# Expert blocks of 128 slots against pairs of 64-slot blocks whose second weights are fetched by number, in a decoder block on one core

## The chip, the core and the metric

The kernel runs on one core of a Trainium2 chip, which has an engine for matrix products (TensorE, PE in the profile), VectorE (DVE), ScalarE (ACT), GpSimd (POOL), and SyncE (SP), which issues most DMAs. Each engine runs its own instructions in order; semaphores connect them. The metric is the time of one execution on the device in microseconds.

## What is computed

One decoder block over 4 sequences of 1024 tokens of 256 numbers: linear attention, cross attention to 77 context tokens, and a feed-forward part (FFN). All 4096 tokens pass a gated FFN with a shared set of weights. 512 of them, given by index lists, also go to one of 8 experts (mixture of experts, MoE): the expert with the best score. Cut to the part that the change touches:

```
x_moe  = x[index_b, index_t]                         # 512 x 256
scores = sigmoid(x_moe @ eg_w.T + eg_b)              # 512 x 8
e      = argmax(scores + exp_bias)                   # an expert for each token
h1, h2 = x_moe @ ew1[e].T + eb1[e], x_moe @ ew2[e].T + eb2[e]
z      = layernorm(silu(h1) * h2) * g + b            # 512 x 128
y      = z @ ew3[e].T + eb3[e]                       # 512 x 256
out[index_b, index_t] = shared_ffn * shared_w + y * expert_w + residual
```

All numbers are float32.

## The kernel before

The first 297 us or so are the two attentions, tile by tile (32 tiles of 128 tokens). Behind them the FFN runs over *units* of four tiles, in the order of `UNITS` (line 43): F0 to F5 (dense units of 512 tokens), G (the 512 gathered tokens through the shared FFN), F6, F7, and the MoE units M0, M1, M2.

The gathered tokens are sorted by expert with rank products and a table. An expert's tokens take whole blocks of 128 slots; the worst case is `NBLK` = MT + NE - 1 = 4 + 7 = 11 blocks, and all 11 are computed always, padded or not. `choose_slots` (DVE) works out each token's slot, POOL scatters the token rows to these slots in memory (line 1761, semaphore `placed`), and SP reads the blocks back into the on-chip memory as `hs_in` (line 475, semaphore `hs_loaded`). `map_blocks` (DVE, a unit behind `choose_slots`) works out `block_i`, the expert's number of each block, and `block_hot`, with which a product adds the expert's bias. All 8 experts' weights (`we_12`, `we_3`) lie on the chip from early on, and PE picks a block's weights by a number that it reads from `block_i` into a register (`load_expert`, line 882: in the program a TENSOR_LOAD and two register instructions).

PE's order in a step q: `gate_products(q)` (for a MoE unit line 753, two products a block with the expert's weights as the moving operand, 256 columns each, and one for the bias, line 755), `z_features(q-1)` and `y_products(q-1)` (line 803, bias line 806), and `to_features(q+1)` (transposes of the next unit's tokens, line 489). At the step of F7 `to_features` of M0 stands at the end; it waits for `hs_loaded[0]`. A float32 product stands in the trace as two passes, so two products are x4 there.

Behind the MoE gate products, ACT makes the tanh (1036), DVE the product with it and the statistics (1322, 1327, 1332, 1336), POOL the reciprocal roots (`invert_blocks`, 1669 and 1672), and DVE normalises (1344). `y_evict` (DVE, 1301) adds the result to a row that other scatters prepared, and `scatter_blocks` (POOL, 1746) writes each block's rows to the output with one indirect DMA a block. The program ends when all of these have landed.

SP's order around it: the stores of the results of F0 to F5 (line 462); then the wait for `placed` and the three loads of `hs_in` (475); then the store of F6, the load of M0's prepared rows (`load_base`, 467), the two stores of F7, and the other loads of prepared rows.

Of the kernel before, what the change touches and what calls it, by code (L numbers as in the profile page):

```python
# [7 lines left out]
BF16 = mybir.dt.bfloat16  # L8
# [5 lines left out]
P = 128  # L14
# [9 lines left out]
HF = 128  # L24
# [15 lines left out]
NBLK = MT + NE - 1  # L40
# [21 lines left out]
def decoder_block(nc, A):  # L62
    ctx = ExitStack()
    with ctx:  # L64
# [143 lines left out]
        hs_in = wide_[:, 0:2816].rearrange("p (b d) -> p b d", b=NBLK)  # L208
# [3 lines left out]
        m_th, m_u, m_z = (wide_[:, n:n + 512].rearrange("p (j n) -> p j n", j=GT) for n in (9792, 10304, 10816))  # L212

# [5 lines left out]
        iota12 = sb("iota12", [P, 12])  # L219
        iota128 = sb("iota128", [P, MT])  # L220
        over = sb("over", [P, NE, MT])
# [7 lines left out]
        past = sb("past", [P, NBLK, NE])  # L229
        block_e = sb("block_e", [P, 12])  # L230
        block_i = sb("block_i", [P, 12], I32)
        block_oh = sb("block_oh", [BIAS_ROWS, NBLK, NE])
        block_sum = sb("block_sum", [BIAS_ROWS, 12])
        block_hot = sb("block_hot", [BIAS_ROWS, 12], BF16)
# [80 lines left out]
        scattered = sem("scattered")  # L315

# [22 lines left out]
        def is_tile(t):  # L339
            return 0 <= t < NT  # L340

# [50 lines left out]
        def _(sp):  # L392
# [94 lines left out]
        def _(pe):  # L487
# [242 lines left out]
            def gate_products(pe, n, half, expert=None, load_expert=None):  # L730
# [15 lines left out]
                else:  # L746
                    k = UNITS[n][1]
                    for j in range(2 * half, min(2 * half + 2, size(n))):
                        b = GT * k + j
                        dst = sbank[2 + half][:, (j % 2) * D:(j % 2 + 1) * D]  # L750
                        for ch in range(CH):
                            w = we_12[:, bass.ds(expert[b], 1), ch, :].rearrange("p o n -> p (o n)")
                            pe.matmul(dst, h3t[:, n % 2, ch, j * P:(j + 1) * P], w, start=(ch == 0), stop=False)  # L753

                        mm = pe.matmul(dst, block_hot[:, b:b + 1].to_broadcast([BIAS_ROWS, P]), be_16[:, 0:2 * HF],  # L755
                                       start=False, stop=True)
# [25 lines left out]
            def y_products(pe, n, expert=None, load_expert=None):  # L782
# [10 lines left out]
                for j in range(size(n)):  # L793

                    if is_moe(n) and j % 2 == 0:
                        wait(pe, ys_ready, GT * UNITS[n][1] - 2 + j)
                    if is_dense(n):
                        w = w_3c[:, :]
                    else:
                        wait(pe, mzt_ready, UNITS[n][1] + 1 + (j >= parts(n)[0][1]))  # L800
# [1039 lines left out]
```

## Time and profile before

| | us |
|---|---|
| median of 3 runs | 381.24 (380.94 to 381.77) |
| the profiled execution's own time | 381.03 |
| its span, first to last instruction | 379.1 |
| outside the span | 1.93 |
| last store of F0 to F5 issued by SP | 334.4 |
| `hs_in` loads issued | 339.46 |
| transposes of M0 on PE | from 343.4 |
| first and last scatter of results on POOL | 361.57 and 375.67 |

The profile is of one execution. A row of the timeline gives start and duration of a run of like instructions on an engine; durations of PE passes overlap their neighbours', so the distance between starts tells the pace. DMA issues count as work of the queue that issues them (SPq); a number given as "to landing" goes from the issue to the arrival.

### The profile page before, as it was taken

What the parts mean: (1) busy time and instruction counts of PE and PEld (TensorE: products, weight loads), DVE (VectorE), ACT (ScalarE), POOL (GpSimd) and SP (SyncE); (2) the same over time, 40 slices, a digit from 0 to 9 for tenths busy, and PEclk for the clock granted to TensorE, in tenths of its full rate; (3) what the DMA queues carried; (4) which work ended last, traced back from release to release, by engine and by line L of the source; (5) the groups of instructions that cost most, each with busy time, mean ns of one, the idle gap of its engine ahead of it and who ended that gap; (6) DMA issues with size and microseconds to landing.
All of it is one profiled execution on the core that took longest, in us unless ns stands there. A gap on an engine that the chain in (4) does not pass through costs nothing. (4 is left out here: it accounts for less than half of the span.)

```text
span 379.1 us, 10587 instructions
## 1 busy us (share of the span) xinstructions
PE 360.7 (95%) x3483; PEld 261.5 (69%) x3483; DVE 298.8 (79%) x934; ACT 164.3 (43%) x395; POOL 282.3 (74%) x417
## 2 busy tenths in 40 slices
PE   8999999999999999999999999999899989998971
PEld 4566677777777777767777777778676566656751
DVE  2588788898989898888898878886756598799771
ACT  1553553453455356436436524432456445341320
POOL 5338987766777866877867789898888888687385
PEclk9999999999999999999999999999999999999997
DMA  8994891300300120032221012003000223136630
GB/s 256 315 310 94 238 298 22 68 16 16 72 30 16 35 54 16 19 83 90 94 52 37 29 24 65 16 22 80 15 30 28 83 86 111 57 115 216 189 109 13
DMA packets 38076, 33.32 MB, mean 88 GB/s; under 512 B 4425, under 2 KB 37224, under 8 KB 38024
## 3 DMA queue, kind: packets, MB, share of 16 engines
q1 hardware_dynamic: 35016, 28.37, 26.4%
q0 software_dynamic: 1456, 3.37, 3.0%
q10 hardware_dynamic: 1552, 0.92, 0.9%
q8 instruction: 29, 0.48, 0.5%
q14 instruction: 23, 0.19, 0.2%
HBM read 15.58 MB, written 13.78 MB: 77 GB/s over the span
## 5 line engine op out<-in xcount | busy, mean ns | idle before, releaser
L1595 POOL TENSOR_TENSOR s_t<-s_t,causal 128x512 f32<-128x512 f32 x63 | 78.9, 1272 | 15.6 <-ACT s_t L909 15.4
L501 PE MATMUL bank<-h1t,w_qkv 128*128 128x512 f32 x112 | 52.9, 595 | 0.4 <-DVE x L1168 0.3
L1155 DVE TENSOR_TENSOR s_t<-sbank,causal 128x512 f32<-128x512 f32 x65 | 43.5, 671 | 1.1 <-PE sbank L522 1.0
L1587 POOL TENSOR_TENSOR state_wide<-state,own_pair 128x256 f32<-128x256 f32 x28 | 18.9, 675 | 25.5 <-DVE state L1146 24.4
L909 ACT ACTIVATE s_t<-sbank 128x512 f32<-128x512 f32 x63 | 33.7, 587 | 7.8 <-PE sbank L522 7.8
L522 PE MATMUL sbank<-arena 32*128 32x256 f32 x512 | 36.7, 400 | 0.0
L561 PE MATMUL bank<-s_t,vp 128*32 128x128 f32 x1024 | 34.6, 275 | 1.1 <-DVE s_t L1155 0.4
L508 PE MATMUL bank<-w_qkv,h1t 128*128 128x256 f32 x128 | 34.2, 389 | 0.0
L1603 POOL TENSOR_TENSOR rr<-ve,neg_half 128x3 f32<-128x3 f32 x36 | 31.9, 887 | 3.0
L646 PE MATMUL bank<-w_out,attn_t 128*128 128x256 f32 x128 | 33.6, 385 | 0.5 <-DVE attn_t L1236 0.5
L740 PE MATMUL sbank<-h1t,w 128*128 128x512 f32 x72 | 33.0, 596 | 0.5 <-ACT h1t L909 0.5
L1190 DVE BATCH_NORM_STATS2 stats<-x 128x6 f32<-128x256 f32 x87 | 31.6, 412 | 0.0
L1112 DVE TENSOR_SCALAR arena<-bank,b_qk 128x512 f32<-128x512 f32 x28 | 21.0, 751 | 13.1 <-PE bank L501 13.1
L909 ACT ACTIVATE prob_t<-bank 77x128 f32<-77x128 f32 x32 | 8.7, 273 | 50.2 <-PE bank L489 50.2
L561 PEld LDWEIGHTS bank<-s_t,vp 128*32 128x32 f32 x1024 | 26.2, 109 | 6.2 <-issue 2.1
L489 PEld LDWEIGHTS bank<-ident,h 128*128 128x128 f32 x128 | 17.6, 140 | 17.3 <-issue 12.4
L501 PEld LDWEIGHTS bank<-h1t,w_qkv 128*128 128x128 f32 x112 | 19.1, 190 | 14.2 <-issue 13.4
L968 ACT ACTIVATE prob<-sc,nmx 128x77 f32<-128x77 f32 x32 | 11.5, 360 | 37.9 <-DVE nmx L1220 37.9
L1614 POOL TENSOR_TENSOR x<-x,b_out 128x256 f32<-128x256 f32 x32 | 26.0, 813 | 0.0
L522 PEld LDWEIGHTS sbank<-arena 32*128 32x128 f32 x512 | 23.1, 184 | 3.9 <-issue 2.4
L646 PEld LDWEIGHTS bank<-w_out,attn_t 128*128 128x128 f32 x128 | 21.8, 190 | 3.5 <-DVE attn_t L1236 1.5
L489 PE MATMUL bank<-ident,h 128*128 128x128 f32 x128 | 24.2, 272 | 0.0
(215 smaller groups left out, 831.7 us busy)
## 6 DMA issues: line engine op xcount, KB each, us to landing
rden_t<-rden SPq DMA_DIRECT2D x64, 64.0 KB
rows<-x SPq DMA_DIRECT2D x32, 128.0 KB, 1.9
x<-in_x SPq DMA_DIRECT2D x7, 512.0 KB, 7.9
out<-x SPq DMA_DIRECT2D x7, 512.0 KB, 2.9
we<-in_we SPq DMA_DIRECT2D x1, 2048.0 KB
rows<-empty SPq DMA_DIRECT2D x1, 1419.0 KB, 6.4
rows<-empty SPq DMA_DIRECT2D x1, 1408.0 KB, 7.6
xmask<-in_mask POOLq DMA_DIRECT2D x2, 616.0 KB, 10.8
```

Of the source, the lines that this page charges most:

```text
L489: return pe.transpose(dst, src, ident[:, :])
L501: mm = pe.matmul(dst[:, :], w_qkv[:, ch, cb * P:(cb + 1) * P], h1t[:, g % 3, ch, :], start=(ch == 0), stop=(ch == CH - 1))
L508: mm = pe.matmul(v_place(t), h1t[:, (t // GT) % 3, ch, tok(t)], w_qkv[:, ch, 2 * D:3 * D], start=(ch == 0), stop=(ch == CH - 1))
L522: mm = pe.matmul(both, kt(slot, ch)[rows, tok(t)], qpair(slot, ch)[rows, :, tok(t)], start=True, stop=True)
L561: mm = pe.matmul(bank[3][32 * r:32 * r + 32, ch * P:(ch + 1) * P], v_of, s_t[:, r, 2 * ch + par, :], start=(first and ch + par == 0), stop ...
L646: mm = pe.matmul(bank[0][:, 0:D], attn_t[:, M % 2, ch, :], w_out[:, ch, :], start=(ch == 0), stop=(ch == CH - 1))
L740: mm = pe.matmul(sbank[2 + half][:, :], w_12[:, ch, half * HF:(half + 1) * HF], h3t[:, n % 2, ch, :], start=(ch == 0), stop=(ch == CH - 1))
L909: return act.activation(dst, src, ACT.Copy)
L1155: dve.tensor_tensor(s_t[:, r, :, :], sbank[r][:, :].rearrange("p (s q) -> p s q", s=4), causal[:, :].unsqueeze(1).to_broadcast([P, 4, P]), ...
L1190: last = dve.bn_stats(stats[:, k, :], x[:, t, :])
L1595: pool.tensor_tensor(s_t[:, r, :, :], s_t[:, r, :, :], causal[:, :].unsqueeze(1).to_broadcast([P, 4, P]), ALU.mult)\
L1603: pool.tensor_tensor(rr[:, i, :], ve[:, i, :], neg_half[:, 0:3], ALU.pow).then_inc(rr_ready, 1)
```

## The change

The unit of an expert's tokens becomes a block of 64 slots: worst case `NHALF` = 2·4 + 7 = 15. Two of them share the 128 partitions of one old block, so `NBLK` is 8 and there are two MoE units, M0 and M1, in place of three. The two halves may have different experts. Each product of a block becomes two products of 64 output partitions (`dst[0:64]` and `dst[64:128]`), which use 64 of the array's columns each: the first with weights picked by number from the resident `we_12` and `we_3`, the second with weights in a buffer of the pair's own, `we_odd[b]`. SP fills the 7 buffers from memory: for each it reads the expert's number from `block_i` into a register and issues two DMAs, 256 KB and 128 KB, whose source addresses come from the register. The buffers lie over tensors that are no longer in use. The tables (`over`, `past`, `block_e`, `block_oh`, ...) get 16 columns in place of 11 or 12. `map_blocks` is split in two functions that are called in a row at the step where it was called before.

```diff
-NBLK = MT + NE - 1
+HB = P // 2
+NHALF = 2 * MT + NE - 1
+NBLK = -(-NHALF // 2)
...
+        def odd_of(k):
+            return [b for b in blocks_of(k) if 2 * b + 1 < NHALF]
...
                 if n == GATHERED:
+                    sp.wait_ge(expert_ready, 1)
+                    for m in range(NMG):
+                        for b in odd_of(m):
+                            e = sp.value_load(block_i[0:1, 2 * b + 1:2 * b + 2], min_val=0, max_val=NE - 1)
+                            sp.dma_start(we_odd[b][:, 0:2 * CH * HF].rearrange("p (c n) -> p c n", c=CH),
+                                         A["we_12"][bass.ds(e, 1), :, :].rearrange("o (c p) n -> p (o c) n", p=P))\
+                                .then_inc(we_odd_in[m], 16)
+                            sp.dma_start(we_odd[b][:, 2 * CH * HF:we_size],
+                                         A["we_3"][bass.ds(e, 1), :, :].rearrange("o p n -> p (o n)"))\
+                                .then_inc(we_odd_in[m], 16)
                     sp.wait_ge(placed, 16 * MT)
...
+                    if half == 0:
+                        pe.wait_ge(we_odd_in[k], 16 * 2 * len(odd_of(k)))
                     for j in range(2 * half, min(2 * half + 2, size(n))):
                         b = GT * k + j
                         dst = sbank[2 + half][:, (j % 2) * D:(j % 2 + 1) * D]
                         for ch in range(CH):
-                            w = we_12[:, bass.ds(expert[b], 1), ch, :].rearrange("p o n -> p (o n)")
-                            pe.matmul(dst, h3t[:, n % 2, ch, j * P:(j + 1) * P], w, start=(ch == 0), stop=False)
...
+                            w = (we_12[:, bass.ds(expert[b], 1), ch, :].rearrange("p o n -> p (o n)"),
+                                 we_odd[b][:, 2 * ch * HF:2 * (ch + 1) * HF])
+                            for o in range(2):
+                                at = slice(j * P + o * HB, j * P + (o + 1) * HB)
+                                pe.matmul(dst[o * HB:(o + 1) * HB, :], h3t[:, n % 2, ch, at], w[o], start=(ch == 0),
+                                          stop=False, skip_group_check=True)
...
-                then_wait(dve.tensor_copy(block_i[:, 0:NBLK], block_e[:, 0:NBLK]))
...
+                dve.tensor_copy(block_i[:, :], block_e[:, :]).then_inc(expert_ready, 1)
...
                 if q == GATHERED + 1:
                     map_blocks()
+                    block_rows()
                     weigh()
```

`y_products` and the bias products change in the same way.

SP, between the stores of F0 to F5 and the store of F6, before:

```order
L462 DMA out<-x 128x4x256 x6
L475 DMA arena<-rows 128x4x256 x2
L475 DMA arena<-rows 128x3x256
L462 DMA out<-x 128x4x256
L467 DMA arena<-rows 128x4x258
```

SP at the same place now. The group from TENSOR_LOAD to the second DMA stands there seven times, once for each odd half block; this is the last one and what follows it (`arena<-in_we` is a fill of `we_odd`, `arena<-rows` at line 502 the load of `hs_in`):

```order
L492 TENSOR_LOAD block_i
L492 ISA x2
L493 ISA
L493 DMA arena<-in_we 128x2x256
L496 ISA
L496 DMA arena<-in_we 128x256
L502 DMA arena<-rows 128x4x256 x2
L479 DMA out<-x 128x4x256
L484 DMA arena<-rows 128x4x258
```

The loads of `hs_in` have moved behind seven reads of a number and fourteen DMA issues, and are two in place of three.

PE, the first transposes of M0 and its first block, before:

```order
L489 MATMUL sbank<-ident,arena 128x128 x8
L489 MATMUL bank<-ident,s_t 128x128 x4
L753 ISA
L753 MATMUL sbank<-we,h1t 128x256
L753 ISA
L753 MATMUL sbank<-we,h1t 128x256
L755 MATMUL sbank<-be,block_hot 128x256
```

PE there now (`w_qkv` is the place of the first odd block's weights):

```order
L516 MATMUL sbank<-ident,arena 128x128 x8
L516 MATMUL bank<-ident,s_t 128x128 x4
L785 ISA
L785 MATMUL sbank<-we,h1t 64x256
L785 MATMUL sbank<-w_qkv,h1t 64x256
L785 ISA
L785 MATMUL sbank<-we,h1t 64x256
L785 MATMUL sbank<-w_qkv,h1t 64x256
L790 MATMUL sbank<-be,block_hot 64x256 x2
```

Each product stands twice, with 64 output partitions in place of 128 and the same 256 moving columns; the order around it is the same.

POOL, the end of its program, before:

```order
L1669 TENSOR_SCALAR m_ve<-g_zmv 128x4
L1672 TENSOR_TENSOR m_r<-m_ve,neg_half 128x4
L1746 DMA out<-arena,token_u 4096x256 x4
L1669 TENSOR_SCALAR m_ve<-g_zmv 128x3
L1672 TENSOR_TENSOR m_r<-m_ve,neg_half 128x3
L1746 DMA out<-arena,token_u 4096x256 x7
```

and now:

```order
L1712 TENSOR_SCALAR m_ve<-g_zmv 128x4
L1715 TENSOR_TENSOR m_r<-m_ve,neg_half 128x4
L1712 TENSOR_SCALAR m_ve<-g_zmv 128x4
L1715 TENSOR_TENSOR m_r<-m_ve,neg_half 128x4
L1789 DMA out<-arena,token_u 4096x256 x8
```

The third unit's roots and three of the eleven scatters are gone.

## Rows read from the trace of the kernel before

**Rows 1.** The page's head: span, and busy time of each engine.
```profile
span 379.1 us, 10587 instructions
PE 360.7 (95%) x3483; PEld 261.5 (69%) x3483; DVE 298.8 (79%) x934; ACT 164.3 (43%) x395; POOL 282.3 (74%) x417
```
**Rows 2.** The chain that ended last: start us, us, engine, tile, line.
```profile
343.77 0.89 PE sbank L489 x8
...
348.12 0.87 PE sbank L753 x4
348.99 0.11 PE sbank L755
...
361.57 1.05 POOL out L1746
...
375.67 0.97 POOL out L1746
```
**Rows 3.** Timeline of POOL at the end: start us, us, then the instruction.
```profile
361.57 1.05 POOL L1746 DMA_INDIRECT out<-arena,token_u  x1 [0.18 <-issue]
362.93 0.97 POOL L1746 DMA_INDIRECT out<-arena,token_u  x1 [0.30 <-issue]
...
366.52 0.19 POOL L1669 TENSOR_SCALAR m_ve<-g_zmv 128x3 f32<-128x3 f32 x1
...
367.88 1.09 POOL L1746 DMA_INDIRECT out<-arena,token_u  x1 [0.20 <-issue]
```
**Rows 4.** SP's DMA issues: line 475's durations and landing, then timeline.
```profile
L475 SPq DMA_DIRECT2D arena<-rows x3: 367/507/509, 339.5 to 340.4; - x3
DMA to landing us min/median/max: 3.8/4.9/5.4
...
3.32 1.53 SPq L394 DMA_DIRECT2D w_qkv<-in_w_qkv  x3
...
62.67 6.45 SPq L432 DMA_DIRECT2D rden_t<-rden  x8
...
339.46 1.47 SPq L475 DMA_DIRECT2D arena<-rows  x3
```
**Rows 5.** Timeline of PE's weight loads ahead of M0's transposes.
```profile
341.28 0.30 PEld L803 LDWEIGHTS bank<-w_3c,s_t 128*128 128x128 f32 x2 [0.59 <-issue]
341.96 0.30 PEld L803 LDWEIGHTS bank<-w_3c,s_t 128*128 128x128 f32 x2 [0.39 <-issue]
...
343.39 1.01 PEld L489 LDWEIGHTS sbank<-ident,arena 128*128 128x128 f32 x8
```
**Rows 6.** Timeline of DVE at the table of experts; SP's wait for the slots.
```profile
337.19 0.17 DVE L1454 CAST block_i<-block_e 128x11 int32<-128x11 f32 x1
...
SPq L475 <- DMA rows<-arena,slot_u: 5.0, 1, 5.0
```
**Rows 7.** Timeline of PE in a step of attention; last row, an expert block's loads.
```profile
203.93 0.61 PE L545 MATMUL bank<-arena,state_wide 128*128 128x128 f32 x4
204.47 1.08 PE L561 MATMUL bank<-s_t,vp 128*32 128x128 f32 x32
...
204.46 0.81 PEld L561 LDWEIGHTS bank<-s_t,vp 128*32 128x32 f32 x32
...
346.87 0.73 PEld L753 LDWEIGHTS sbank<-we,h1t 128*128 128x128 f32 x4
```
**Rows 8.** PE's first and last work; stretches behind it (clock third from last).
```profile
0.99 5.80 PE L843 MATMUL sbank<-ones 128*128 128x512 bf16 x14 [0.99 <-POOL ones L1696]
...
371.23 0.27 PE L806 MATMUL bank<-be,block_hot 72*128 72x256 bf16 x1
...
374.00:374.50 0.50, 0.00 (x0) 0.00 (x0) 0.00 (x0) 0.00 (x0) 0.20 (x2) 1.00 0.00 0
...
375.00:375.50 0.50, 0.00 (x0) 0.00 (x0) 0.00 (x0) 0.00 (x0) 0.36 (x1) 0.50 0.00 0
```
**Rows 9.** Stretch while `hs_in` arrives; last three numbers: clock, DMA share, GB/s.
```profile
343.00:345.00 2.00, 2.00 (x16) 1.71 (x14) 1.90 (x15) 0.32 (x1) 1.92 (x2) 1.00 1.10 357
```

More of the change, by code:

```diff
@@ L207, in decoder_block @@
         wide_ = arena[:, :, :].rearrange("p s n -> p (s n)")
[L208 removed]
+        hs_in = wide_[:, 0:2048].rearrange("p (b d) -> p b d", b=NBLK)
         res = wide_[:, 2816:2816 + NBLK * BW].rearrange("p (b d) -> p b d", b=NBLK)
@@ L218, in decoder_block @@
         one1 = sb("one1", [P, 1])
-        iota12 = sb("iota12", [P, 12])
-        iota128 = sb("iota128", [P, MT])
-        over = sb("over", [P, NE, MT])
+        iota16 = sb("iota16", [P, 2 * NBLK])
+        iota64 = sb("iota64", [P, 2 * MT])
+        over = sb("over", [P, NE, 2 * MT])
         blocks = sb("blocks", [P, NE])
@@ L228, in decoder_block @@
         slot_y = sb("slot_y", [P, MT], U32)
[L229 to L234, printed above, removed]
+        past = sb("past", [P, 2 * NBLK, NE])
+        block_e = sb("block_e", [P, 2 * NBLK])
+        block_i = sb("block_i", [P, 2 * NBLK], I32)
+        block_oh = sb("block_oh", [BIAS_ROWS, 2 * NBLK, NE])
+        block_sum = sb("block_sum", [BIAS_ROWS, 2 * NBLK])
+        block_hot = sb("block_hot", [BIAS_ROWS, 2 * NBLK], BF16)
         m_ve = sb("m_ve", [P, GT])
@@ L315, in decoder_block @@
         scattered = sem("scattered")
+        expert_ready = sem("expert_ready")
+        we_odd_in = [sem(f"we_odd_in{k}") for k in range(NMG)]
         x_v = A["x"].rearrange("(g j p) d -> g p j d", p=P, j=GT)
@@ L751, in gate_products @@
                         for ch in range(CH):
-                            w = we_12[:, bass.ds(expert[b], 1), ch, :].rearrange("p o n -> p (o n)")
-                            pe.matmul(dst, h3t[:, n % 2, ch, j * P:(j + 1) * P], w, start=(ch == 0), stop=False)
-                        mm = pe.matmul(dst, block_hot[:, b:b + 1].to_broadcast([BIAS_ROWS, P]), be_16[:, 0:2 * HF],
-                                       start=False, stop=True)
+                            w = (we_12[:, bass.ds(expert[b], 1), ch, :].rearrange("p o n -> p (o n)"),
[4 more added lines that the diff above has]
+                                          stop=False, skip_group_check=True)
+                        for o in range(2):
+                            hot = block_hot[:, 2 * b + o:2 * b + o + 1].to_broadcast([BIAS_ROWS, HB])
+                            mm = pe.matmul(dst[o * HB:(o + 1) * HB, :], hot, be_16[:, 0:2 * HF],
+                                           start=False, stop=True, skip_group_check=True)
                         if j + 1 < size(n):
@@ L881, in load_expert @@
                 if b < NBLK:
-                    expert.append(pe.value_load(block_i[0:1, b:b + 1], min_val=0, max_val=NE - 1))
+                    expert.append(pe.value_load(block_i[0:1, 2 * b:2 * b + 1], min_val=0, max_val=NE - 1))
             for q in range(3, NU + 1):
@@ L1430, in choose_slots @@
                 total = bank[3][:, MT * NE:(MT + 1) * NE]
-                then_wait(dve.tensor_tensor(over[:, :, :], total.unsqueeze(2).to_broadcast([P, NE, MT]),
-                                            iota128[:, :].unsqueeze(1).to_broadcast([P, NE, MT]), ALU.is_gt))
+                then_wait(dve.tensor_tensor(over[:, :, :], total.unsqueeze(2).to_broadcast([P, NE, 2 * MT]),
+                                            iota64[:, :].unsqueeze(1).to_broadcast([P, NE, 2 * MT]), ALU.is_gt))
                 then_wait(dve.tensor_reduce(blocks[:, :], over[:, :, :], mybir.AxisListType.X, ALU.add))
@@ L1464, in weigh @@
+                then_wait(dve.tensor_reduce(block_sum[:, :], block_oh[:, :, :], mybir.AxisListType.X, ALU.add))
+                dve.tensor_copy(block_hot[:, :], block_sum[:, :]).then_inc(block_ready, 1)
             def weigh():
```

53 lines of the change are left out of this document (32 added, 21 removed).

## The prediction

> **What bounds the kernel now.** I read the page's head, then the chain that ended last, then the timelines of POOL, SP and PE over the last 45 us, and last the views that price single operations. The head puts PE at 95% of the 379.1 us [rows 1], but that is an average; the change touches nothing before 337 us, so what counts is which wait ends last from there. The chain says it: from M0's transposes at 343.77 it runs on PE through the gate products of M0 and M1, by way of DVE's statistics and POOL's roots to the first scatter of results at 361.57, and from there on POOL to the last one at 375.67 [rows 2]. Two ends are to be seen. At its head stands a DMA: SP had idled 5.0 us for the slots [rows 6], issued the load of `hs_in` at 339.46, and the first of its three landed 3.8 us later, at 343.26 [rows 4]; PE loads its first weights for M0 at 343.39 [rows 5]. So M0's start has no slack against that load. At its tail stands POOL, whose scatters follow each other every 1.28 us or so, with the third unit's roots between [rows 3].
>
> **The third unit.** POOL's scatters start at 361.57 and 362.93, 1.36 apart, and from there every 1.28 (the last of eleven starts at 375.67) [rows 2, 3]. Three fewer save 3 × 1.28 = 3.8. The roots of M2 and what goes with them cost the distance from 366.52 to 367.88 = 1.4 [rows 3]; a scatter would start there with the usual gap, so 1.3 of it goes. Sum 5.1. What is next late is M1's own results: PE has no gate products of M2 between, so its y products come earlier than before, and before they were already in time. The eight scatters then stay back to back, and the last starts 7 × 1.28 behind the first plus 0.1. Gain on the path: **5.1 us**. The reads of three expert numbers on PE and the store of 11 blocks of zeros against 8 lie beside other work: nothing.
>
> **The table.** `block_i` is there at 337.36 [rows 6]. Two of the four operations ahead of it grow from 88 to 128 columns and the others from 11 to 16; from their durations of 0.2 each that is below 0.15 in all. SP can start at 337.5. `block_hot` is later by as little, and PE's dense products cover it. The table is made no later or earlier than before.
>
> **SP's new work, and what is queued behind it.** SP is free then, and it has seven groups of a read and two DMA issues before it comes to `hs_in`. An issue: three 256 KB weight loads took 1.53, 0.51 each; line 475's shortest took 0.37; eight `rden` copies, with more and smaller pieces, took 6.45, 0.81 each [rows 4]. I take 0.51, since it is the same shape of source and destination. No row of this trace shows an address from a register on SP; the same 0.51 is assumed for it, with 0.81 as the upper end. A read of a number: on PE, between pairs of weight loads with one read between them, the distance is 341.96 − 341.28 = 0.68 [rows 5]. A pass and its load need little of the sequencer: 32 of each were issued in 0.9 [rows 7], so four instructions are 0.06 and the read with its two register instructions is 0.62. The lower end for it is nothing. The Trainium skill (DMA: Bandwidth & Descriptors, Latency and other measured facts) gives a `tensor_load` a floor of about 0.6; no row shows one on SP.
>
> So the stretch is 7 × (0.62 + 2 × 0.51) = **11.5 us**, between 14 × 0.37 = 5.2 and 7 × (0.68 + 2 × 0.81) = 16.1. The slots are placed long before its end. The bytes don't set it: 7 × 384 KB = 2.75 MB at the 357 GB/s of [rows 9] are 7.7 us, and the transfers run beside the issues. `hs_in` is issued at 337.5 + 11.5 = 349.0 in place of 339.46, lands 3.8 later at 352.8, and PE starts M0 at 352.9 in place of 343.39: **9.5 us later**. No other engine can go around it: PE stands in order at M0's transposes, and behind them wait the z and y products of F7, whose results DVE and POOL need before the stores, and all of M0 and M1. SP's wait for F6's store is in the same queue, but that store is needed by nobody before the scatters. M0's own odd weights are issued in the first four groups, and have landed when PE asks for them.
>
> **Pairs of products.** An expert block takes 0.87 + 0.11 = 0.98 of PE's chain [rows 2]. Now it has twice the products at the same number of moving columns, each on half of the array's columns. The nearest row is attention's numerators: 32 passes of 128 moving columns on a quarter of the columns each start at 204.47, and the next work starts 0.9 later, 28 ns a pass. The four passes on the full array before them, with the same 128 moving columns, start 0.54 ahead, 135 ns a pass [rows 7]. So four quarters ran side by side, and I take it that two halves do: no cost. The other end is no overlap: 0.98 for each of 8 blocks, 7.8. Weight loads: a 32-column load took 0.81 / 32 = 25 ns, so a 64-column one is an estimated 51 ns, and eight are 0.4 against 0.73 for four full ones [rows 7]. The passes still set the pace.
>
> In the same rows the array goes from full to quarter columns with no gap beyond 0.1. The Trainium skill (TensorEngine Tiling (Array Packing), Key Properties) says that changing the tiling mode drains the array. There are some eight such changes on the path here; by a drain as long as the 0.1 that the rows leave room for, the result would be 0.8 later. I leave it out of the sum.
>
> **The clock.** PE finishes F6's y products at about 343.6 and would idle 9.3 us. Behind its last product at 371.5 the granted clock is 1.00 up to 374.5 and 0.50 from 375.0 on [rows 8], so the stall ends at the lower level, 1.2 GHz. How soon it is back: the kernel's first 14 products of 512 bf16 columns took 5.80, 0.41 each [rows 8], which is the pace of 1.2 GHz, under steady work. For 5.4 us behind the stall PE then does half of what it did: transposes (0.9 more), a wait for ACT's eviction (unchanged), and some 1.3 us worth of gate products (1.3 more). **2.2 us**, between none and some 5 if all of M0's four blocks run slow too.
>
> **The sum**, on the span: 379.1 − 5.1 + 9.5 + 2.2 = 385.7. The profiled execution's time was 381.03 and its span 379.1, so 1.93 lies outside, and it is 0.2 under the median. 385.7 + 1.93 = **387.6 us**, 1.7% slower.
>
> **Rivals.** (A) *SP's stretch is short, and the change is faster.* The total change is −5.1 + (S − 2.0) + clock, with S the stretch: M0 moves by S less the 2.0 between the table and the old issue. It turns at S = 7.1 without a clock cost; to be faster by over 0.8 us, S must be under 6.3, or 0.9 a group. Two issues alone are 1.02, so the reads would have to be free and issues near their shortest. At S = 5.2 the stall is 3.2 us, too short for the clock: 379.1 − 5.1 + 3.2 + 1.93 = 379.1 us. For it speaks only that 0.37 does stand in a row. 9%, with 4% more for a time that can't be told from no change.
>
> (B) *SP's groups are longer*, because an address from a register costs: S = 16.1 gives 14.1 for the 9.5, and the clock stays low for M0, some 5: 379.1 − 5.1 + 14.1 + 5 + 1.93 = 395.0. For it: no row shows such an address. Against: PE picks its weights by register at an unchanged pace. 12%.
>
> (C) *The halves don't run side by side.* The 7.8 comes on top: 395.4. Against it stand the numerators. 5%.
>
> (D) *The load of `hs_in` was not what held M0*, and only the gain shows: 376 and less. It would need PE to be late for a later load, which 343.26 and 343.39 exclude. Under 1%, held in A.
>
> **The numbers.** My forecast has 70%: 387.6, and by its own terms (S from 10 to 14, the clock from 0.5 to 3.5) 384.5 to 391.5. With 17% for B and C above and 13% for A and no change below, the range that leaves out 2 in 10 is 384.0 to 392.0. A measurement of this kernel can tell about 0.2%, 0.8 us, from no change. Faster 0.09, same 0.04, slower 0.87.
>
> **What would show it.** SP's timeline: fourteen issues from 337.5 with a group's period of 1.6, `hs_in` issued near 349. PE: a gap of some 9 us before M0's transposes that ends with a DMA, and the clock at 0.50 near its end. Behind it the same order as now, with 0.98 to 1.0 a block once the clock is back. POOL: eight scatters 1.28 apart, the last 9.1 behind the first. From M0's transposes to the first scatter 17.8 us, as now, plus the clock's. I am wrong if SP's groups have a period under 1.0, if PE doesn't wait there, or if a block takes near 2.

## The result, and the profile of the changed kernel

The changed kernel took 390.44 us (median of 4 runs, 389.97 to 390.93) against 381.28 for the kernel before: a ratio of 1.0239, with an interval of 1.0220 to 1.0259. It is slower, by 9.2 us. I had said 387.6, from 384.0 to 392.0. The profiled execution took 390.07 with a span of 388.2.

The page's head, to be laid beside [rows 1]:

```profile
span 388.2 us, 10638 instructions
PE 358.9 (92%) x3514; PEld 257.6 (66%) x3514; DVE 295.4 (76%) x917; ACT 162.2 (42%) x390; POOL 278.3 (72%) x412
```

PE is busy for less time than before, and the span is 9.1 us longer. PE's waits say where (engine, tile and line, what it waited for, us in total, times, longest):

```profile
PE sbank L516 <- DMA arena<-rows: 12.1, 1, 12.1
```

One wait, for one load, of 12.1 us. The chain that ended last shows what is in front of it and behind it (start us, us, engine, tile, line), to be laid beside [rows 2]:

```profile
350.46 5.45 DMA arena<-rows
...
356.05 1.96 PE sbank L516 x8
...
358.52 0.60 ACT h1t L949
...
359.26 1.98 PE sbank L785 x8
361.23 0.21 PE sbank L790 x2
361.44 0.86 PE sbank L785 x8
362.31 0.11 PE sbank L790 x2
...
364.37 1.02 PE sbank L516 x8
365.40 1.73 PE bank L834 x8
367.13 1.01 PE sbank L785 x8
...
375.86 1.05 POOL out L1789
...
384.93 0.98 POOL out L1789
```

SP's timeline (start us, us, then the instruction) is where the 12.1 us come from. DVE has written `block_i` by 337.62. Then the groups of a read and two issues follow, and `hs_in` behind them, where [rows 4] had it at 339.46:

```profile
338.70 0.33 SPq L493 DMA_DIRECT2D w_qkv<-in_we  x1
339.21 0.36 SPq L496 DMA_DIRECT2D w_qkv<-in_we  x1
340.34 0.38 SPq L493 DMA_DIRECT2D w_qkv<-in_we  x1
340.91 0.34 SPq L496 DMA_DIRECT2D w_qkv<-in_we  x1
...
347.04 0.38 SPq L493 DMA_DIRECT2D arena<-in_we  x1
347.94 0.35 SPq L496 DMA_DIRECT2D arena<-in_we  x1
349.51 0.38 SPq L493 DMA_DIRECT2D arena<-in_we  x1
350.07 0.34 SPq L496 DMA_DIRECT2D arena<-in_we  x1
350.46 1.18 SPq L502 DMA_DIRECT2D arena<-rows  x2
```

The difference to the kernel before, in order, on the spans (M0's first transposes stood at 343.60 in PE's timeline before):

| stretch | before | after | difference | predicted |
|---|---|---|---|---|
| to the start of M0's transposes | 343.60 | 356.05 | +12.45 | +9.5 |
| from there to the first scatter | 17.97 | 19.81 | +1.84 | +2.2 |
| first scatter to last | 14.10 | 9.07 | −5.03 | −5.1 |
| sum | | | +9.3 | +6.6 |

The spans differ by 9.1, because what follows the last scatter is 0.16 shorter. So two of the three terms came out within 0.4 us, and the first is 2.95 short.

### The profile page after: what moved, and what is told of

Same layout as the page of the kernel before. It is cut to its first block and busy times, and to the rows that moved or that the text cites. A ratio compares the mean times of both kernels' runs of the same rounds, so it can differ in the third digit from the quotient of the medians.

```text
span 388.2 us, 10638 instructions
## 1 busy us (share of the span) xinstructions
PE 358.9 (92%) x3514; PEld 257.6 (66%) x3514; DVE 295.4 (76%) x917; ACT 162.2 (42%) x390; POOL 278.3 (72%) x412
## 5 line engine op out<-in xcount | busy, mean ns | idle before, releaser
L1008 ACT ACTIVATE prob<-sc,nmx 128x77 f32<-128x77 f32 x32 | 11.5, 360 | 37.9 <-DVE nmx L1260 37.9
```

## The experiments

My theory was that the delay of `hs_in` in SP's queue is the whole loss, that the third unit's end is a gain of 5 us whatever else happens, and that the halves of a block cost nothing. The rival was that something else of the change (the pairs, the fills' traffic, the waits for the second weights) costs as much, and that `hs_in` only hides it. Unless it is said otherwise, the load of `hs_in` is M0's, and its landing is the time from its issue to its end. The kernels' times stand beside medians of the kernel before on the same chip.

### The load of hs_in ahead of the fills

```diff
                 if n == GATHERED:
+                    sp.wait_ge(placed, 16 * MT)
+                    for m in range(NMG):
+                        b = blocks_of(m)
+                        sp.dma_start(hs_in[:, b.start:b.stop, :], ...).then_inc(hs_loaded[m], 16)
                     sp.wait_ge(expert_ready, 1)
...
-                    sp.wait_ge(placed, 16 * MT)
-                    for m in range(NMG):
-                        b = blocks_of(m)
-                        sp.dma_start(hs_in[:, b.start:b.stop, :], ...).then_inc(hs_loaded[m], 16)
```

> SP waits for the slots and issues the two loads of hs_in first, then the seven groups of a read and two fills. Nothing else is changed. Theory (the loss is the place of hs_in in SP's queue): hs_in is issued at about 339.5 again and M0's transposes start at 343.4 to 343.6. The stall moves to M0's gate products, which wait for four groups of 1.66 us and their landing: about 340.5 + 6.6 + 2.5 = 349.6 in place of 345.9, so 3.7 late, plus 0 to 2 for the clock, less 5.1 for the third unit: 380.0 to 382.5 us. Rival (pairs of half products or 2.75 MB of fills cost the time): no better than 388.

Measured: 383.10 (382.52 to 383.71) against 381.63, a ratio of 1.0045 (1.0030 to 1.0059): 0.6 above the range that the theory gave, and far from the rival's 388. The order of four lines on one queue is worth 7.3 of the 9.2 us (7.7, if each kernel is taken against its own runs of the kernel before). That the load was what held M0 is thereby shown, and by how much. PE's timeline shows what took its place:

```profile
344.09 1.04 PE L516 MATMUL sbank<-ident,arena 128*128 128x128 f32 x8
...
351.15 0.68 PE L785 MATMUL sbank<-we,h1t 128*64 x1 [5.58 <-DMA vp<-in_we]
```

The transposes start at 344.09, 0.5 behind where they were. But M0's odd weights now wait for the slots: the fourth group of fills is issued at 346.91 and 347.47, and its last piece lands 3.2 later. PE waits 5.6 us for it, until 351.15, where 349.6 was expected. The first scatter stands at 368.71, 7.1 later than before, the tail gives 5.0 back, and the rest is the loss of 1.5 to 2. So neither order of these two things on SP wins: the time of seven groups is paid in front of one or the other.

### Fixed experts, their weights fetched early

This takes the reads and the fills off the critical stretch altogether. The weights are those of fixed experts, fetched at the fourth unit, so it computes with other weights; pairs of products and the missing third unit remain.

```diff
-                if n == GATHERED:
-                    sp.wait_ge(expert_ready, 1)
+                if n == 4:
                     for m in range(NMG):
                         for b in odd_of(m):
-                            e = sp.value_load(block_i[0:1, 2 * b + 1:2 * b + 2], ...)
                             sp.dma_start(we_odd[b][...],
-                                         A["we_12"][bass.ds(e, 1), :, :]...)
+                                         A["we_12"][b:b + 1, :, :]...)
```

> The seven buffers are filled with the weights of fixed experts (number b for buffer b), without a read of a number, ahead of the store of F4's results, long before they are used: the odd halves are computed with a wrong expert's weights. The products, their number and sizes are as in the changed kernel. Theory: what is left is the gain of the third unit, 381.2 - 5.1 = 376.1 us (375.5 to 376.8), with M0's transposes at 343.4. Rival (half products in pairs cost on PE): 0.5 to 1 us a block, 379 us or more.

Measured: 377.76 (377.62 to 379.07) against 381.63, a ratio of 0.9899 (0.9882 to 0.9915): a gain of 3.9, of the 5 that the tail holds; 375.5 to 376.8 was expected. In PE's timeline the two halves of a product start 0.01 apart, the next pair 0.21 later, and a block with its bias product fills 349.56 to 350.64 with nothing idle:

```profile
349.56 0.38 PE L784 MATMUL sbank<-we,h1t 128*64 x1
349.58 0.38 PE L784 MATMUL sbank<-vp,h1t 128*64 128x256 f32 x1
349.78 0.38 PE L784 MATMUL sbank<-we,h1t 128*64 x1
349.79 0.38 PE L784 MATMUL sbank<-vp,h1t 128*64 128x256 f32 x1
```

The profiled execution was the slowest of the four, 1.3 above the median, and its span is only 1.8 shorter than before. M0's transposes start at 344.29, 0.7 later than before; from there to the first scatter are 20.11 in place of 17.97; the tail is 4.5 shorter. The 2.1 in the middle are on ACT (the last bracket is its idle time before, and what ended it):

```profile
353.07 0.38 ACT L1075 ACTIVATE arena<-sbank 128x256 f32<-128x256 f32 x1 [3.33 <-remote]
```

This `tanh` needs the products that ended at 350.7, and starts 2.4 us after them. The profile names no releaser in this kernel ("remote"). In the kernel before the corresponding one starts within 0.1 of the end of its products. The other three executions may have lost less. I come back to it below.

### PE kept busy through the stall

Forty-eight products of ones, into a bank that is free at that time, stand ahead of M0's transposes, to hold the clock up. They are work that the kernel doesn't need.

```diff
                 if q == FIRST_M - 1:
+                    wait(pe, z_ready, dense(q + 1))
+                    wait(pe, th_ready, dense(q + 1))
+                    for _ in range(48):
+                        pe.matmul(sbank[3][:, :], ones16[:, :],
+                                  ones16[:, 0:1].to_broadcast([P, 512]), start=True, stop=True)
                     to_features(pe, q + 1)
```

> The changed kernel with 48 products of 512 bf16 columns of ones in PE's stall ahead of M0's transposes, written to a bank that is read by nobody then. 48 x 0.213 = 10.2 us, which ends inside the stall of 12.5 us. Theory (the lower clock behind the stall costs 2.0 us, the distance from M0's transposes to the first scatter having grown from 17.8 to 19.8): that distance is 17.8 again, and the time 388.2 to 388.8 in place of 390.4. Rival (the 2 us come from changing between full and half array columns, or from the products): no change, 390.4.

Measured: 390.66 (389.38 to 392.89) against 381.63, 1.0257 (1.0220 to 1.0295): no faster than the changed kernel, where 388.2 to 388.8 was expected, and with a wide spread. Yet it answers its question. From M0's transposes, at 356.73 here, to the first scatter at 374.68 are 17.95 us, against 19.81 in the changed kernel and 17.97 before. So the clock costs 1.9 us, and on balance nothing else in that stretch costs anything. The windows show the clock itself (start and end, length, then busy time and instructions of PE, PEld, DVE, ACT, POOL, then clock, DMA share, GB/s), first in the changed kernel:

```profile
349.00:351.00 2.00, 0.00 (x0) 0.00 (x0) 0.00 (x0) 0.00 (x0) 1.39 (x3) 0.50 0.95 303
...
356.00:359.00 3.00, 2.79 (x12) 2.42 (x12) 0.12 (x1) 0.97 (x2) 0.00 (x0) 0.50 1.07 376
359.00:361.00 2.00, 1.74 (x8) 0.98 (x10) 1.05 (x8) 0.12 (x1) 0.77 (x2) 0.50 0.38 126
361.00:363.00 2.00, 2.00 (x22) 1.47 (x20) 0.13 (x1) 0.38 (x1) 0.46 (x1) 0.92 0.04 8
```

and in the one with the products of ones:

```profile
356.00:358.00 2.00, 1.27 (x12) 1.29 (x12) 0.00 (x0) 0.17 (x1) 0.00 (x0) 1.00 1.08 379
```

Part of what it won there, it lost at the other end: its `hs_in` was issued at 350.00, 0.5 sooner than in the changed kernel, and landed 6.6 us later, where it was 5.5, so the transposes start 0.7 later. The tail is 0.4 longer as well, and the span of this execution, the fastest of the four, is 387.4 against 388.2. Why the other three took longer, their times don't tell. That a landing can move by so much was new to me; the next five kernels are about it.

### What makes the landing long

Two theories stood against each other. One: the bytes of the fills, 2.75 MB, hold the queues when `hs_in` is issued. The other: not the bytes but another burst, the write of F7's prepared rows by POOL's scatters or F6's store, which in the kernel before came after `hs_in` had landed. The first of these runs leaves most of the fills' bytes out (16 of 128 partitions, so the second weights are not there).

```diff
-                            sp.dma_start(we_odd[b][:, 0:2 * CH * HF]...,
-                                         A["we_12"][bass.ds(e, 1), :, :]...)
+                            sp.dma_start(we_odd[b][0:16, 0:2 * CH * HF]...,
+                                         A["we_12"][bass.ds(e, 1), :, :]...[0:16])
```

> The changed kernel with fills of 16 of 128 partitions, an eighth of the bytes: fourteen issues and seven reads stay. The other partitions of the odd weights hold old data, so the odd halves are computed with wrong weights. Theory (hs_in landed 5.5 us behind its issue in place of 3.8 because fills were queued ahead of it): M0's transposes start 3.8 to 4.0 behind the issue, 1.5 earlier, and the time is 388.7 to 389.2. Rival (the 5.5 comes from the scatters of prepared rows that run at the same time): 390.4. If the issues themselves get cheaper with the bytes, hs_in is issued before 350 and it is less than 388.5.

Measured: 388.88 (388.66 to 390.22) against 381.63, 1.0203 (1.0183 to 1.0223). The groups have a period of 1.6 in place of 1.66, `hs_in` is issued at 348.80, and still

```profile
DMA to landing us min/median/max: 5.9/6.4/6.9
```

(DMA issue to landing of line 502's two loads). So the bytes of the fills explain neither the 12.1 nor the 5.5 us. The time lies in the range that the theory gave, but not for its reason: the load is issued 1.66 sooner, and its landing is no shorter.

The next run leaves the fills whole, and takes the reads and registers away: the experts are fixed numbers, at the same place of the queue behind the same wait.

```diff
                         for b in odd_of(m):
-                            e = sp.value_load(block_i[0:1, 2 * b + 1:2 * b + 2], ...)
                             sp.dma_start(we_odd[b][...],
-                                         A["we_12"][bass.ds(e, 1), :, :]...)
+                                         A["we_12"][b:b + 1, :, :]...)
```

> The changed kernel with the fourteen fills at their place and of their size, but from fixed experts (number b for buffer b): the seven reads of a number and the address from a register are gone, and the odd halves are computed with a wrong expert's weights. Theory (a group of 1.66 us is 0.8 of read and register work and 0.9 of two issues): the seven groups take 7 x 0.9 = 6.3 us, hs_in is issued near 344.5 in place of 350.5, and the time is 383.3 to 385. Rival (the issues pace themselves by the bytes, 2.75 MB at 350 GB/s = 7.9 us, or by the queue): the groups take 8 us or more, and the time is above 385.5.

Measured: 384.78 (384.21 to 385.18) against 381.42, 1.0083 (1.0067 to 1.0098), as expected. The fourteen issues stand back to back from 338.47, and SP comes to `hs_in` 5.1 us sooner than in the changed kernel:

```profile
338.47 0.38 SPq L492 DMA_DIRECT2D w_qkv<-in_we  x1
338.90 0.46 SPq L495 DMA_DIRECT2D w_qkv<-in_we  x1
339.41 0.45 SPq L492 DMA_DIRECT2D w_qkv<-in_we  x1
...
345.40 0.98 SPq L501 DMA_DIRECT2D arena<-rows  x2
```

A group is 0.99 us without its read, and 1.66 with it. The reads and the registers are thus 0.67 a group on the path. And the landing is 6.0 us here, with whole fills closely behind each other ahead of it and the scatters and the store beside it. The DMA engines are full from 345 to 349 (share 1.04 to 1.06 at 343 GB/s), as [rows 9] had them in 2 us in which `hs_in` arrived.

Then POOL's part: the table of the bases, and with it the scatters of F7's rows, one unit later.

```diff
-                if q == GATHERED + 2:
+                if q == GATHERED + 3:
                     place_bases()
```

> The changed kernel with the four scatters of prepared rows (by the slots, 346.8 to 351.6 on GpSimd) a unit later, behind the roots of M0, so that they don't run while hs_in is under way. Theory (these scatters made hs_in land 5.5 to 6 us behind its issue instead of 3.8; an eighth of the fills' bytes did not help): M0's transposes start 3.8 to 4.3 behind the issue, and the time is 388.5 to 389.2 in place of 390.4. Rival (it is the read of rows itself, or the store of F6's results right behind it): 5.5 again, and 390.4 or more.

Measured: 395.44 (394.65 to 397.99) against 381.42, 1.0381 (1.0346 to 1.0416). The theory fell here. `hs_in` was issued at 349.46 and landed after 6.9 us, longer than ever, though the DMA engines were not full for most of that time (share 0.67 from 351 to 353 and 0.88 from 353 to 355). The kernel's time says nothing about it, because the edit made the results' first scatter wait 3.7 us for F7's store, which had become the later one:

```profile
381.38 1.05 POOL L1789 DMA_INDIRECT out<-arena,token_u  x1 [3.75 <-DMA out<-x]
```

F6's store stands right behind `hs_in` on SP. I moved it behind the first load of bases:

```diff
                 if n == FIRST_M - 1:
                     load_base(0)
-                if what == "F":
+                if n == FIRST_M - 1:
+                    store_out(UNITS[n - 1][1])
+                if what == "F" and n != FIRST_M - 2:
                     store_out(k)
```

> The changed kernel with the store of F6's results moved on SP behind the load of M0's prepared rows (to about 356.5), so that it isn't issued right behind hs_in. Theory (the store beside it made hs_in land 5.5 to 6.9 us behind its issue instead of 3.8): M0's transposes start 3.8 to 4.3 behind the issue, and the time is 388.7 to 389.3 in place of 390.4. Rival (neither this store, nor the fills' bytes, nor the scatters by themselves): 5.5 or more again, and 390.4.

Measured: 390.46 (388.90 to 391.35) against 380.83, 1.0256 (1.0232 to 1.0281); landing

```profile
DMA to landing us min/median/max: 4.9/5.6/6.2
```

The landing is 0.6 shorter than the 5.5, which is less than the 1.1 by which it differs between two kernels with the same transfers (the changed one and the one with the products of ones), and the time is the rival's 390.4. So taking away any one of the three does not bring the 3.8 back. The last run of this row takes all three away at once:

```diff
-                            sp.dma_start(we_odd[b][:, 0:2 * CH * HF]...,
+                            sp.dma_start(we_odd[b][0:16, 0:2 * CH * HF]...,
...
+                if n == FIRST_M - 1:
+                    store_out(UNITS[n - 1][1])
...
-                if q == GATHERED + 2:
+                if q == GATHERED + 3:
```

> The changed kernel with three edits at once: fills of an eighth of the bytes (wrong weights for the odd halves), the scatters of prepared rows a unit later, and the store of F6's results behind the load of M0's prepared rows. hs_in is then the only large transfer from its issue at about 349 on. The late scatters make the whole time longer, near 394; what counts is the landing. Theory (its longer way came from traffic beside it, each part of which is enough to slow it): it lands 3.8 to 4.0 behind its issue. Rival (something that comes with the stall or the reads of numbers, not with traffic): 5 or more.

One run was made: 394.45 against 381.14, with the late bases' own loss in it. Line 502 and PE's timeline:

```profile
349.05 0.97 SPq L502 DMA_DIRECT2D arena<-rows  x2
...
DMA to landing us min/median/max: 3.9/4.3/4.8
```

```profile
353.04 1.94 PE L518 MATMUL sbank<-ident,arena 128*128 128x128 f32 x8 [9.54 <-DMA arena<-rows]
```

3.9 us, which is what it was in the kernel before. The issue is as late as ever (349.05), and the stall falls from 12.1 to 9.5. So, by this one execution, the landing is long because of what moves beside it, and with one of the three taken away the other two keep it at 4.9 or more. The two versions of the next section have fills alone beside it, and 4.7 and 4.8; no run has the scatters or the store alone, so what each of them does stays open. One table of all the runs:

| kernel | beside `hs_in` | issue to landing, us |
|---|---|---|
| before | nothing of the three | 3.8 |
| hs_in ahead of the fills | the first fills, from 1.9 behind its issue | 3.8 |
| fixed experts, early | fills long done | 3.8 |
| all three taken away | 16-partition fills only | 3.9 |
| one issue a fill (below) | one fill ahead, three behind | 4.7 |
| the same with copies on ACT (below) | one fill ahead, three behind | 4.8 |
| late store | fills, POOL's scatters | 4.9 |
| changed kernel | fills, scatters, store | 5.5 |
| small fills | scatters, store | 5.9 |
| fixed experts, same place | fills back to back, scatters, store | 6.0 |
| products of ones | fills, scatters, store | 6.6 |
| late bases | fills, store | 6.9 |

The order within the rows from 4.7 on isn't explained by what is beside them: the late bases have the scatters away and the longest landing. Between the changed kernel and the one with the products of ones, whose transfers are the same, lie 1.1 us, so a difference of that size is not read as an effect here.

### A version that pays for fewer groups in front

If the price is by group on SP, and both orders lose, then groups should be cheaper and only what M0's first block needs should be ahead of `hs_in`. The three weights of an expert lie in one array here, prepared outside the kernel as the others are, so a fill is one issue of 384 KB. On SP stand: one fill, the wait for the slots, M0's `hs_in`, three fills, M1's `hs_in`, three fills. PE waits for the second weights by two blocks, not by unit.

```diff
+                    def fill(b):
+                        e = sp.value_load(block_i[0:1, 2 * b + 1:2 * b + 2], ...)
+                        sp.dma_start(we_odd[b][:, :], A["we_all"][bass.ds(e, 1), :, :]...)\
+                            .then_inc(we_odd_in[b // 2], 16)
...
+                    sp.wait_ge(expert_ready, 1)
+                    fill(odd[0])
+                    sp.wait_ge(placed, 16 * MT)
+                    blocks_in(0)
+                    for b in odd[1:4]:
+                        fill(b)
+                    blocks_in(1)
+                    for b in odd[4:]:
+                        fill(b)
```

> A version meant to keep the gain: both weight tensors of an expert also lie side by side in memory, so that a buffer is filled by one DMA of 384 KB; SP fills the first buffer while it would wait for the slots, then issues M0's hs_in, then the fills of the other three buffers of M0, M1's hs_in, and the rest; PE waits for two buffers at a time. Theory (what cost time was the place and length of SP's groups): M0's transposes start at 343.4, no gate product waits for weights by more than 0.5, and the time is 376.2 us (375.7 to 377.2), less than both. Rival (the fills' bytes hold up hs_in or the products): PE waits 1 to 2 us at M0's second half, and it is 378 or more. As in the run with weights filled early, 1.2 us can go to a wait of ScalarE for its code.

Measured: 378.62 (377.72 to 379.02) against 381.42, 0.9919 (0.9905 to 0.9933): faster than both kernels, though 375.7 to 377.2 was expected. `hs_in` is issued at 339.62 and PE waits 0.5 for it; the weights make nobody wait. Against the kernel before, M0's transposes start 0.9 later (344.48), the stretch to the first scatter is 1.6 longer (19.58), and the tail is 4.7 shorter. The 1.6 are again on ACT, where the products it waits for had ended at 349.0:

```profile
351.85 0.38 ACT L1079 ACTIVATE arena<-sbank 128x256 f32<-128x256 f32 x1 [5.18 <-remote]
```

That is 2.9 us without a named cause. Here it is M0's first `tanh`; in the run with fixed experts it was the second, and the first stood only 0.6 with its input ready. In both, no other engine has work outstanding that it needs, and DMA is moving data beside it (224 GB/s from 349 to 351 with fixed experts). My reading was that ACT's next piece of code had to be fetched at that moment. If so, the place is a matter of how many instructions stand in front of it. The last version has sixteen copies of two columns into a scratch tile on ACT, behind the exponential of the weights of pairs, two units earlier, where ACT is idle:

```diff
                     act.activation(pair_e[:, :, :], pair_d[:, :, :], ACT.Exp).then_inc(pair_exp, 1)
+                    for s_ in range(16):
+                        act.activation(scratch[:, 2 * s_:2 * s_ + 2], parity[:, :], ACT.Copy)
```

> The version with one DMA a buffer, with 16 copies of 2 columns added on ScalarE behind the exponentials of the mixing weights, where it idles for 5 us. In that version ScalarE made M0's first tanh 2.9 us after its products were done, with no engine named as what it waited for, and GpSimd's first scatter came at 364.1 in place of 361.6. Theory (ScalarE waits there for a piece of its code, which comes slowly while SP's DMAs fill the queues): sixteen more instructions move the piece's start to an idle place, the tanh follows its products by 0.1, and the time is 376.2 to 376.8. Rival (a wait that belongs to this tanh, or to the products before it): the 2.9 stays, and 378.6.

Measured: 377.14 (376.95 to 377.47) against 380.83, a ratio of 0.9900 (0.9884 to 0.9917), 0.3 above the expected range. The wait is gone and the `tanh` follows its products, though DMA is busy there (share 0.97, 369 GB/s):

```profile
349.41 0.38 ACT L1080 ACTIVATE arena<-sbank 128x256 f32<-128x256 f32 x1 [2.35 <-PE sbank L794]
```

```profile
349.00:351.00 2.00, 2.00 (x24) 1.34 (x20) 1.67 (x9) 0.38 (x1) 1.39 (x3) 1.00 0.97 369
```

The first scatter is at 362.96 and the last at 372.07, in a span of 375.4: M0 1.27 later than before, the stretch behind it 18.09, the tail 5.0 shorter. That adds up to 3.6 on the span, and the medians differ by 3.7. Between this version and the one without the copies the ratios' intervals overlap, and they ran on different chips, so that the copies make it faster isn't shown by the times; that they take the wait away is shown by the trace of one execution of each. That the wait was a fetch of code is not shown, and the traces speak against it. Packets that carry instructions stand as a kind of their own among the DMA queues (queue and kind, packets, MB, share). In the version without the copies, from 349 to 353, while ACT stands until 351.85, there are none, and none starts from 334.5 to 353 either:

```profile
q1 hardware_dynamic: 688, 1.27, 85.5%
q0 software_dynamic: 91, 0.26, 16.2%
```

With fixed experts one of 16 KB starts in the half microsecond from 350.5 and takes 1.3, and ACT stands 1.2 beyond its end; one like it starts between 353.0 and 353.5 in the kernel before, where no `tanh` of ACT is late. So the cause of the wait stays open.

## Why the prediction was right, and where it was short

**What bounds the kernel.** Right. M0's start had no slack against `hs_in`, and the end was POOL's scatters. Both ends moved as told: the load's wait went from nothing to 12.1, and the first experiment gave 7.3 us back by the order alone. The middle of the forecast was 2.8 too low, though: the number is inside the range because the range had room for a stretch of 14 on SP. In the terms of the sum, 2.95 of delay was missing, and the clock's term was 0.36 too high.

**The third unit.** 5.1 was predicted; 5.03 was measured (375.86 to 384.93 against [rows 2]). The eight scatters are 1.28 to 1.36 apart as before. M1's results were in time for them. In the other kernels with eight scatters the tail takes 9.02 to 9.56, a gain of 4.5 to 5.1.

**The table.** It was to be later by less than 0.15. `block_i` is ready 0.26 later than in [rows 6]:

```profile
337.45 0.17 DVE L1494 CAST block_i<-block_e 128x16 int32<-128x16 f32 x1
```

Of that, only 0.10 is the table: from its first operation to `block_i` are 1.00 (from 336.62), and 0.90 before (from 336.46). The other 0.16 is that DVE came to it later. So the estimate of the table held.

**SP's stretch.** This is one of the two terms that were mis-sized. I had 11.5 from 337.5 on, and it was 12.8 from 337.65 to 350.46. A group's period of 1.64 was predicted and 1.66 measured for five of them, but that is luck, as two errors cancel: an issue takes 0.33 to 0.38 (two with what lies between them 0.9, not 1.02), and what is left for the read and its registers is 0.77 (from 341.25, the end of one group's issue, to 342.02), not 0.62. The last two took longer: from the fifth group's start to the seventh's, 345.35 to 349.51, are 4.16 us where two periods are 3.3. In the other kernels with seven such groups of whole or small fills it is 3.57 to 4.20, and 4.11 in the first experiment, where they come 3 us later; so it belongs to the place in the program more than to the time. What it is, no run here settles. In each of these seven kernels a packet of 8 KB that carries instructions starts within 0.5 of the seventh group's first issue; in the kernel before, and in the run at the same place without reads, none of this queue (q14) does between 338 and 354:

```profile
q14 instruction: 1, 0.01, 1.0%
```

(changed kernel, 349 to 351). That the two belong together is a guess. With 0.3 more in the first group that makes the 1.3. Without the reads the period falls from 1.66 to 0.99, so a read with its registers is 0.67 on the path here. The Trainium skill (DMA: Bandwidth & Descriptors, Latency and other measured facts) gives a `tensor_load` a floor of about 0.6. This trace doesn't show that as the instruction's own time: five of the seven TENSOR_LOAD rows on SP are 0.27, the first is 0.47 and the last 0.72. By the page's figure alone, as an estimate, the seven groups would be 0.5 less than by the 0.67.

**The landing of hs_in.** The second mis-sized term, and here the step itself was at fault. "Lands 3.8 later" was taken over from the kernel before, and the sentence that the fills' bytes don't set the stretch was right about the stretch and silent about the landing. It was 5.5. With nearly all neighbouring traffic away it is 3.9 again. What I had missed is that the load of `hs_in` in its old place had beside it only the loads of the other units' blocks, and that I moved it among fourteen fills, POOL's scatters and a store. A hint stood in my own rows, since [rows 9] showed a share of 1.10 while those loads arrived; but full engines are not the whole of it, as the late bases show. The range had no room of its own for this term.

Together: the issue came 1.46 later than the 349.0 of the sum, and the landing was 1.65 longer. That is 3.1, against the 2.95 that the first line of the table is short; the rest is that it counts from M0's first product and the prediction from its first weight load.

**Pairs of products.** The number is right, no cost, and in part by luck. The halves do run side by side, 0.01 apart. Behind M0's first block, from 361.44 to the end of M1's last product at 371.94, PE needs 10.50 us, and before it needed 10.50 as well (347.14 to 357.64). In detail the chain does show something that I had left out of the sum. Transposes behind pairs take 1.02 where they took 0.88, and pairs behind work on the full array 1.01, twice, where it was 0.86 and 0.90. The Trainium skill (TensorEngine Tiling (Array Packing), Key Properties) has the array drained when the tiling mode changes; that agrees with these three, at 0.11 to 0.15 each. Together they cost 0.40. It doesn't show in the 10.50 because M1's last four transposes take 0.59 where they took 1.00, which my sum did not have; the kernel with the products of ones shows the same (1.02, 1.01 and 1.01, and 0.58). Had these transposes been as before, the pairs would have cost 0.4. I had estimated 0.8 for drains at eight changes, at 0.1 each; the three that the chain shows fit that size. That it is a drain is the page's word; the rows show only the longer times.

**The clock.** 2.2 predicted, 1.9 measured, in two ways: by the run whose PE was kept busy (17.95 against 19.81), and in the chain, where the transposes took 1.96 for 0.89 and the first block 1.98 for 1.13, together 1.92. ACT's eviction between them is 0.60 in both, as I had said. That 5.4 us at the lower level was so near to this kernel's 5.3 (356.05 to 361.3) is luck: in the other kernels with such a stall the granted clock was back at 1.00 from 2.8 to 6.1 us behind PE's restart, and the stretch to the first scatter took 18.82 (no reads), 19.35 (small fills) and 19.68 (late store).

**The rivals.** A needed a group under 0.9; a group without any read is 0.99. So even fixed numbers would not have made this order a win, and the run that has them lost 3.4 us. B had the right sign, at a third of its size, but not its reason: it wanted issues of up to 0.81 because of an address from a register, and they took 0.33 to 0.38. What was longer is the read with its registers, and the first and the last two groups. C is refuted by the trace of every kernel.

## What to carry to other kernels

When a wait on a value that comes late is put on a queue, everything behind it on that queue is late by the wait and by all that the value is used for: price it by what the next thing in the queue holds up, and put the load that somebody waits for ahead, or only as much of the new work as its first user needs. A load that is moved keeps its size but not its landing time; before it is taken from the old trace, look at what will be in flight beside it. One transfer per value read in place of two, one fill ahead of the load and the rest behind it, and waits by two blocks made the difference between a loss of 2.4% and a gain of 0.8% here (1.0% with the copies on ACT). No run separates these three; with the two transfers, moving all fills behind the load left a loss of 0.45%.

## What the runs showed of the hardware that was not expected

- A load of `hs_in` (512 KB) took 3.8 to 3.9 us from issue to landing with little beside it, 4.7 and 4.8 among fills alone, and 4.9 to 6.9 when two or three of fills, indirect scatters and a store ran beside it. Taking one of the three away did not bring the 3.8 back.
- A read of a number on SP with its registers cost 0.67 to 0.77 us in front of two issues of 0.33 to 0.38 each; the TENSOR_LOAD in it took 0.27 in five of seven. Of seven such groups the last two took together 0.4 to 0.9 us longer in every kernel that had them.
- ACT stood 2.4 and 2.9 us with its input ready and no releaser named, in two kernels whose other waits had gone. In one of them, sixteen instructions more in front of it made it go away; the wait held no packet of instructions.
- The granted clock was back at 1.00 some 5 us after PE had taken up work again in the changed kernel (from 356.05 to 361.3), and the same work took 1.9 us more; in the other kernels with a stall it was back after 2.8 to 6.1 us.
